# Two attention layers on one core: attention in steps of 512 tokens instead of 256, with four PSUM banks used in turn

## What is computed

```python
# layer 0: attention between channels of one head (32 by 32), y = ctx
q, k, v = Wq@y + bq, Wk@y + bk, Wv@x + bv            # 256 x 2048 each, 8 heads of 32 channels
attn = softmax(einsum('bhdl,bhel->bhde', q, k) / sqrt(256))
o = Wo @ (attn @ v) + bo + x
x = group_norm(o) * gn_w + gn_b                      # one mean and variance for a sample
# layer 1: attention between the 64 tokens of a chunk, 8 heads, q, k and v all from ctx
scores = einsum('bnqhd,bnkhd->bnhqk', qh, kh) / sqrt(32) + where(mask > 0, 0, -1e9)
out = softmax(scores) @ vh                           # then W_out, bias, times mask
out = out + x
return (out - mean(out)) * rsqrt(var(out) + 1e-5)    # over the tokens of a channel
```

## Time and profile before

| | |
|---|---|
| median of 3 executions | 1542.44 us (1541.51 to 1542.45) |
| profiled execution, its own time | 1542.93 us |
| its span, first to last instruction | 1541.1 us |
| PE busy | 1511.2 us, 98% |
| DVE busy | 1278.6 us, 83% |
| ACT busy | 1108.9 us, 72% |
| POOL busy | 450.8 us, 29% |
| granted TensorE clock, mean | 0.995 of full speed |

### The profile page before, as it was taken

The page is one execution under the profiler, slowest core; times in us unless marked ns, Lnnn a source line. Parts: engine busy times, 40 slices in busy tenths (PEclk is TensorE's granted clock), DMA queues, the critical chain, the costliest instruction groups (busy, mean ns, idle before and its releaser), DMA issues.

```text
span 1541.1 us, 54826 instructions
## 1 busy us (share of the span) xinstructions
PE 1511.2 (98%) x24146; PEld 1274.8 (83%) x24146; DVE 1278.6 (83%) x2024; ACT 1108.9 (72%) x2064; POOL 450.8 (29%) x294
## 2 busy tenths in 40 slices
PE   9999999999999999999999999999999999999995
PEld 6888888888888888888888888888888888888883
DVE  5778888888788887978879888888888889788897
ACT  6667676777767777677776776867767776777765
POOL 1114133141331413314142141422314133141321
PEclk9999999999999999999999999999999999999998
DMA  7232331423315233142422414233142331524212
GB/s 250 56 99 83 111 124 38 152 84 118 111 36 152 84 118 111 54 148 71 143 86 84 132 57 145 84 111 121 55 151 78 120 116 41 149 83 129 59 49 91
DMA packets 96397, 157.28 MB, mean 102 GB/s; under 512 B 5408, under 2 KB 38304, under 8 KB 96032
## 3 DMA queue, kind: packets, MB, share of 16 engines
q1 hardware_dynamic: 96160, 153.78, 31.8%
HBM read 120.20 MB, written 33.55 MB: 100 GB/s over the span
## 4 chain that ended last, share of the span: by engine, by line
PE 96%; DVE 1%; ACT 1%; issue 1%; POOL 0%; ACTq 0%; POOLq 0%; DVEq 0%
PE pj_ps L313 46%; PE l_ps L313 12%; PE s_ps L328 9%; PE w_ps L339 8%; PE l_ps L424 7%; PE w_ps L357 7%; PE l_ps L441 2%; PE l_ps L468 2%; PE l_ps L462 1%; PE l_ps L471 1%; PE s_ps L499 0%; PE l_ps L450 0%; DVE o_sb L972 0%; PE l_ps L432 0%; PE l_ps L489 0%
## 5 line engine op out<-in xcount | busy, mean ns | idle before, releaser
L1132 POOL TENSOR_TENSOR prob<-prob,row_inv 128x1024 f32<-128x1024 f32 x128 | 257.9, 2015 | 890.4 <-DVE row_inv L864 890.4
L671 ACT CAST att_hi<-w_ps 128x256 fp32r<-128x256 f32 x256 | 83.2, 380 | 192.2 <-PE w_ps L357 192.1
L313 PE MATMUL pj_ps<-y_hi,w_hi 128*128 128x512 f32 x510 | 207.4, 407 | 0.0
L313 PE MATMUL pj_ps<-y_hi,w_lo 128*128 128x512 f32 x510 | 202.0, 396 | 0.0
L313 PE MATMUL pj_ps<-y_lo,w_hi 128*128 128x512 f32 x510 | 202.0, 396 | 0.0
L859 DVE TENSOR_REDUCE row_sum<-prob 128x16 f32<-128x1024 f32 x128 | 155.0, 1211 | 49.2 <-ACT prob L640 49.1
L847 DVE TENSOR_REDUCE row_max<-s_ps 128x16 f32<-128x1024 f32 x128 | 155.6, 1215 | 21.2 <-PE s_ps L328 21.2
L328 PEld LDWEIGHTS s_ps<-k_s,q_s 32*64 32x64 f32 x8192 | 130.8, 133 | 43.1 <-issue 35.2
L1149 POOL TENSOR_TENSOR o_sb<-o_sb,u_sb 128x1024 f32<-128x1024 f32 x60 | 157.7, 2638 | 0.9
L854 DVE TENSOR_TENSOR prob<-s_ps,row_max 128x1024 f32<-128x1024 f32 x128 | 155.6, 1215 | 0.1
L635 ACT COPY prob_t<-w_ps 128x512 f32<-128x512 f32 x256 | 152.2, 596 | 3.8 <-PE w_ps L339 3.1
(11 more groups left out here) (139 smaller groups left out, 3552.2 us busy)
## 6 DMA issues: line engine op xcount, KB each, us to landing
y_raw<-in_ctx SPq DMA_DIRECT2D x64, 512.0 KB, 4.9
yt_raw<-in_ctx_t SPq DMA_DIRECT2D x64, 512.0 KB, 4.6
x_raw<-in_x SPq DMA_DIRECT2D x64, 512.0 KB, 5.1
out_z<-o_sb SPq DMA_DIRECT2D x60, 512.0 KB, 3.6
mask_b<-in_mask SPq DMA_DIRECT2D x64, 256.0 KB, 4.0
out_z<-o_sb SPq DMA_DIRECT2D x8, 256.0 KB, 2.7
u_sb<-in_w SPq DMA_DIRECT2D x2, 512.0 KB, 5.8
w_sb<-in_w SPq DMA_DIRECT2D x1, 1024.0 KB, 10.7
```

The lines of the kernel that those rows point to most:

```text
L313: last = mm(dst, lhs, rhs, start=i == 0, stop=i == len(todo) - 1)
L1132: nc.gpsimd.tensor_tensor(cut, cut, row_inv[:, u % 2, :].unsqueeze(2).to_broadcast([P, 2 * HEADS, CHUNK]), ALU.mult).then_inc(probs_done, 1)
```

## The change

Attention of layer 1 goes by blocks of 512 tokens, 4 in a sample.

- `s_ps` has four banks and `w_ps` is gone. The same four banks hold in turn the mask and scores, the transposed probabilities and (banks 0 and 1) the values. So the scores of block `b+1` must have left a bank before the transposes of block `b` go into it, and the values of `b` must have left banks 0 and 1 before the mask of `b+2` goes in.
- Each row tile `i` of the scores has a bank of its own, and all eight places (4 row tiles by 2 column halves) are used in turn. Scores are 64 products in a row on PE, values 64; the two no longer stand side by side.
- `q_s`, `k_s`, `att_hi`, `att_lo` have one buffer instead of two; `blocked` is made for the two halves of partitions apart, in two instructions of 64 partitions.
- The queues of all engines are written in another order. One of four final normalisations of a sample (`result(n, 1)`) goes from DVE to ACT; the final shift is made with the negated mean in every sample, one small DVE instruction more.

```diff
-        s_ps = es.enter_context(nc.psum_tensor("s_ps", [P, 2, 2, HALVES, 2, CHUNK], F32))
-        w_ps = es.enter_context(nc.psum_tensor("w_ps", [P, 2, 512], F32))
+        s_ps = es.enter_context(nc.psum_tensor("s_ps", [P, HP, QUADS, HALVES, 2, CHUNK], F32))
+        pt_ps = s_ps[:, :, :, :, :, :].rearrange("p i f g c k -> p i f g (c k)")
+        av_ps = s_ps[:, 0:2].rearrange("p c f g e k -> p c (f g e k)").rearrange("p c (g j q) -> p c g j q", g=HALVES, j=PAIRS)
...
+            def scores(n, b):
+                pe.wait_ge(qkv_copied, count(n, 24, 6 * b + 3))
+                pe.wait_ge(mask_set, count(n, 8, 2 * b + 1))
+                for f in range(QUADS):
                     for g in range(HALVES):
-                        for i in range(4):
-                            r, h = divmod(i, 2)
-                            rows = slice(DH * i, DH * i + DH)
-                            last = mm(s_ps[64 * h:64 * h + 64, r, t // 2, g, t % 2, :], q_s[rows, b % 2, g, cut], k_s[rows, b % 2, g, cut],
+                        for c in range(2):
+                            for h in range(2):
+                                t = 4 * f + 2 * h + c
+                                cut = slice(t * CHUNK, (t + 1) * CHUNK)
+                                for i in range(HP):
+                                    rows = slice(DH * i, DH * i + DH)
+                                    last = mm(s_ps[64 * h:64 * h + 64, i, f, g, c, :], q_s[rows, g, cut], k_s[rows, g, cut],
                                       start=False, stop=True, skip_group_check=True)
...
+            def transpose(n, b, e):
+                pe.wait_ge(probs_done, count(n, 8, 2 * b + e))
+                if n == SAMPLES - 1 and b == BLOCKS - 1:
+                    pe.wait_ge(att_lo_done, count(n, 4, b - 1))
+                else:
+                    pe.wait_ge(shifted, count(n, 8, 2 * (b + 1) + e))
...
+            def values(n, b):
+                pe.wait_ge(qkv_copied, count(n, 24, 6 * b + 5))
+                pe.wait_ge(pt_copied, count(n, 16, 4 * b + 3))
...
+                elif e == 0:
+                    act.wait_ge(att_lo_done, count(n, 4, b - 2))
+                else:
+                    act.wait_ge(pt_copied, count(n, 16, 4 * (b - 2) + 3))
...
+                    behind = not (first and b == 0)
+                    if j == 0:
+                        if behind:
+                            transpose(n, b - 1, 0)
+                        if ahead:
+                            qk(n, b + 1, Q_W, 0)
+                        if behind:
+                            transpose(n, b - 1, 1)
+                        if s == S_MX:
+                            layer0_output(n, 0)
+                        if ahead:
+                            qk(n, b + 1, Q_W, 1)
+                        if s == S_GRAM[2]:
+                            gram_part(n, 2)
+                        if s == 0 and not first:
+                            mean_over_partitions(n - 1)
+                        if behind:
+                            values(n, b - 1)
+                        if s == 0 and not first:
+                            variance_over_partitions(n - 1)
+                        if s == S_MX:
+                            layer0_output(n, 1)
+                    elif j == 1:
+                        if ahead:
+                            qk(n, b + 1, K_W, 0)
+                        if s == S_GRAM[0]:
+                            gram_part(n, 0)
+                        if ahead:
+                            qk(n, b + 1, K_W, 1)
+                        if s == S_GRAM[3]:
+                            gram_part(n, 3)
+                    elif j == 2:
+                        if ahead:
+                            v(n, b + 1, 0)
+                        if s == S_MX + 2:
+                            layer0_output(n, 2)
+                        if behind:
+                            wout(n, b - 1, 0)
+                        if s == S_GRAM[1]:
+                            gram_part(n, 1)
+                        if s == S_HLT:
+                            layer0(n, s)
+                        if ahead:
+                            scores(n, b + 1)
+                        if s == S_MX + 2:
+                            layer0_output(n, 3)
+                    else:
+                        if ahead:
+                            v(n, b + 1, 1)
+                        if s == S_SUM:
+                            layer0(n, s)
+                        if behind:
+                            wout(n, b - 1, 1)
+                    if s not in (S_HLT, S_SUM):
+                        layer0(n, s)
```

566 lines of the change are left out of this document (288 added, 278 removed).

## The result

The changed kernel takes 1557.82 us (median of 7 runs, 1549.93 to 1563.34) beside 1541.51 us for the kernel before (7 runs, 1539.99 to 1544.0). The ratio is 1.0098, with a 95% interval of 1.0069 to 1.0126: 1% slower, where 1505 us was forecast and 1545 was the upper end. The profiled execution took 1561.99 us, its span is 1560.2.

The account below looks back on a forecast made before the run. PE's queue was taken as the bound: 1541.1 - 71.7 (faster scores and values) + 35 (new waits) = 1504.4 us of span, given as 1505 us after small corrections; 8 in 10 range 1465 to 1545.

Parts of the forecast that it names:

- So the time is the sum of PE's queue: Whole kernel: PE busy 1511 of 1541 us, so only less PE work helps and any PE wait hurts.
- Values and scores 1.51 us each, −72 us: Attention blocks: each run of 64 takes 1.51 us, a block 3.02 instead of 4.14, 72 us over 64 blocks.
- Places, not banks: Scores: four places set 29 ns a product; eight would allow 15 ns, leaving issue at 17 to 20 ns.
- four-place rival: Scores gain nothing from eight places: 28 us less work, 18 us of waits, 1531 us; chance 0.16.
- Transposes even: Attention blocks: 16 transposes before and after, 0.88 us for eight, no gain and no loss.
- New waits for DVE and ACT, +35 us, 0 to 75: PE waits on the shared banks' chain and late DVE work: 2.3 us a sample, 35 over 15 samples.
- four places named: PE waits at `a_wide` (0 to 1 us), `m_lo` (0.6), slot 6's Gram sum (0.3), slot 0's group variance (0.5).
- hardly any wait: Whole kernel: the work saving holds with almost no new PE waits, 1472 us; chance 0.13.
- First and last samples even: First and last samples: reordered too, taken as neither gain nor loss, within 5 us.
- DVE the pacemaker, 1577: Scores to transposes: DVE idles 18.3 us a sample and sets the pace, losing 36 us; chance 0.15.
- mixtures between 1541 and 1560: Whole kernel: mixtures of the four-place scores and DVE pacemaker cases, 1541 to 1560 us; chance 0.06.
- What would show it: Profile after: score groups starting within 1.1 to 1.3 us, PE under 97% with DVE-ended waits, DVE 84 to 87% busy.

Follow-up runs that it names:

- e16: Changed kernel with six trials of small products put first, two waits each, as separate instructions or joined to products; one run, 1716.82 us.
- e13: Changed kernel without PE waits that another wait implies, the transposes' two waits swapped, product order unchanged; 1497.09 us, ratio 0.9713 to the kernel before.
- e8: Changed kernel with the stores of samples 0 to 14 cut to 16 of 512 columns; 1543.71 us, ratio 1.0019 to the kernel before.
- e7: Changed kernel with the values in one run behind the first K projection, ACT's k copy before its values copy; 1551.36 us, 1.0068.
- e10: Changed kernel with values behind the first K projection, ACT's first-sample order changed, and more reordering on DVE, ACT and PE; 1536.47 us, 0.9974.
- e18: Kernel before the change, with PE waits that another wait implies taken out, no order changed; 1539.18 us, ratio 0.9983.

## Why the prediction was wrong

**The mechanism.** PE gets its instructions in packets of 256. A run of 64 small products is exactly 256 instructions and uses them up in 1.4 to 1.5 us. The packet behind must have been asked for early. Where PE stands at a wait that is an instruction of its own soon behind a packet's border, the transfer can start about 1 us after the wait ends, and so later than without it [e16]. In the changed kernel the 28 stalls over 0.7 us had a transfer that started 3.6 us (median) behind the border of the packet before, 1.1 us for the packets that caused none. That the separate waits are necessary for the loss is shown by e13, which changes nothing but waits; that separate waits can hold the transfer back is shown by e16. The length of the run is not what changed: before, 32 scores and 32 values stood back to back, also 256 instructions, in 1.88 us. What changed is their pace, 1.42 to 1.52 us, and what stands around them. The stores have a share too [e8], by which way is not shown.

**By the prediction's own steps.**

- *"So the time is the sum of PE's queue, and the change can only help by making that sum smaller; it hurts wherever it makes PE wait."* This step failed. The queue of instructions itself is a supply that can run dry. A sign stood in the trace before: the 5.1 us of issue in 8 places, all in the values, and "issue 1%" in the earlier trace rows. I gave it no price. It is a term of +44 us of idle time. About 16 us more is the difference between the 52 us saved (next point) and the 36 seen in PE's busy time; it fits the stretches at the low clock, and e13, without the stalls, has 20.1 us less busy time than the changed kernel.
- *Values and scores 1.51 us each, −72 us.* The direction is right, the size too large. Scores take 1.377 from first to last start and 1.524 to the next product, values 1.270 and 1.416 (forecast 1.19 to the last start). By these medians at full clock that is 52 us less; by the means of e13, with the few stalls and slow stretches of either kernel counted, 58. "17 to 20 ns a product" was 21.5 for scores.
- *Places, not banks.* Right: 0.91 us for 32 on eight places, 1.16 on four. The 29 ns of the earlier trace rows on four places became 21.5 on eight, so the four-place rival (1531) fell. By the Trainium skill (TensorE: Matmul & The Clock Gate, section "Wait — 56ns, not 53.3ns?") starts never come closer than about 25 ns. The trace again disagrees: here 128 records start within 1.377 us, 10.8 ns apart and 21.5 a product.
- *Transposes even.* Right by starts: from the first of eight to the next product it is 0.79 us in both kernels.
- *New waits for DVE and ACT, +35 us, 0 to 75.* The steady samples of the changed kernel show little of them: `yt_hl` 3.2 us. With the stalls gone they are still only about 7 (e13: 4.7 and 2.5), so the price was about five times too high. Of the four places named, only the Gram half (`yt_hl`) waits, about as forecast; `x_lo` was not named, and `a_wide`, the variance and `m_lo` wait in steady samples only once orders are changed (e7 about 21 us with `yt_hl`, e10 11.2). DVE does come 2.2 us late to the maxima of one block a sample, as forecast, in the changed kernel and in e13; the step that failed here is that PE would wait for it behind them. Nearest is the "hardly any wait" rival (1472).
- *First and last samples even.* Failed: +12.3 us, 7.2 in e13. The rows name it: ACT's queue ahead of `q_s` 4.5 once, and the last samples' one buffer for `att_lo` 5.6 once.
- *DVE the pacemaker, 1577, and mixtures between 1541 and 1560.* The time came out in the band that was given 0.06, for another reason than either case it mixes: that is chance. DVE is 81% busy, less than before, and PE waits for it in few places.
- *What would show it.* PE under 97% was seen, but ended by issue, not DVE; DVE at 84 to 87% was 81, and 84 in e13.

With the missing term taken away, the sum holds better than its parts, which is luck, as two errors cancel: 1504.4 us of span was forecast and e13 has 1495.4. Less was saved (14 less) and less waited for (28 less), with 7 more at the two ends; 2 us are left unassigned.

**Open.** Which instruction of a packet asks for the next one: waits up to some 80 to 90 instructions behind the border went with late packets, one at 110 did not. Seven of the 28 stalls in the changed kernel, 11.4 of their 45.1 us, have no separate wait in the packet before; e13 has none of these stalls either, and why they went is not shown. Where a wait does stand ahead, the transfer started 2.0 us (median) after its end, not 1.0 as in e16; how much of that is the traffic was not separated. Nor is it shown why the old kernel, with as many separate waits and runs as long, had only 5.1 us of stalls: the pace of the runs and the place of the waits both changed. The spread of the changed kernel's runs (13 us, against 2 in e13) fits packets that race with traffic, but that is argued, not shown.

## What to carry to other kernels

When a run of small instructions is made faster or put in another place, count instructions and not only time: here a run of one packet (256 instructions in 1.5 us) made PE depend on when the next packet was asked for. Drop every wait on the busiest engine that another wait implies, and look in the trace for waits that are instructions of their own; they show in no busy time. Idle time put down to "issue" in the middle of a run of like products deserves a price, even at 5 us. Here curing it by moving work around cost more than removing the waits.

## What the runs showed of the hardware

- PE's instructions came in 16,384-byte packets of 256; a packet moved for 1.0 us (median; 0.88 to 2.34), and in a bare long run one came per 3.45 us.
- 32 products of 32x64 by 64 took 0.91 us on eight places, 1.16 on four, 2.08 on two, 3.94 on one. Where the banks were varied, with four places and with two, they made no difference.
- Of two waits before a matmul one was an instruction of 51 ns on PE's load queue, counted in no busy time. In the old kernel taking such waits out gained 2.5 us (e18), in the changed one 61 us (e13).
- Behind nine of the 17 stalls of 1.5 to 2.7 us the granted clock fell to the low level. Behind one of them, eight products of L439 and the next start took 3.1 us; at the full clock in e13 they took 1.7.
- Leaving out some 30 MB of stores was worth nothing in one kernel (ratio 1.0001) and 14 us in the other.
